# First edge stretch of a two-part graph kernel: stores of packed sums on two queues, each step's mix in two halves

## The chip, the cores and the metric

The kernel runs on one core of one Trainium2 chip. The metric is the device time of one execution in microseconds (us), as the median of several runs.

## What is computed

The input is 50,000 nodes with 128 features and 50,000 edges sorted by destination. The first part is a graph attention layer with four heads (below), then a normalisation over all nodes, an ELU, a residual and a layer norm. The second part is two relational layers over the same edges. The change touches the edge work of the first part alone.

```python
src = jnp.concatenate([edge_index[0], loop]); dst = jnp.concatenate([edge_index[1], loop])
xl = (x @ Wl).reshape(n, H, C);  xr = (x @ Wr).reshape(n, H, C)
m = xl[src] + xr[dst]
logits = jnp.einsum('ehc,hc->eh', jax.nn.leaky_relu(m, 0.2), att)
amax = jax.ops.segment_max(logits, dst, num_segments=n)
ex = jnp.exp(logits - amax[dst])
denom = jax.ops.segment_sum(ex, dst, num_segments=n)
out = jax.ops.segment_sum((ex / (denom[dst] + 1e-16))[:, :, None] * xl[src], dst, num_segments=n)
```

## The kernel before

The program is written by hand, one instruction list for each engine, with semaphores between them; the order of the lists is the order of the code. The work runs in stages. In the first, the node projections xl and xr are made for all nodes and written to DRAM; then comes the stretch that the change is about, the first edge stretch.

The edges are cut into four chains (`CHAINS`) of 100 (`ROWS`) tiles of 125 (`TE`). The stretch is a loop of 100 steps; step i takes tile i of each of the four chains. What one step does, by engine:

- GpSimd gathers the source rows of xl, one indirect transfer for each chain (L879), up to six steps ahead. It waits until `values` of six steps earlier has read the buffer.
- SyncE's queue loads four windows of 224 rows of xr (`load_windows`, L457 for the addresses, L461 for the transfers), three steps ahead; a step's buffers come free when its mix is done. Every fourth step it also loads a block of two tables (L618, L621). Then it stores the packed sums of an earlier step (`save_sums`, L429 for the addresses, L644 for the four transfers of 125 rows of 137 floats). The store of a chain waits until the store of the same chain a step earlier has landed (semaphore `ew_out`), since neighbouring tiles overlap in DRAM and the later one must win.
- TensorE runs `mix(i+1)`: for each chain one transpose of the gathered rows (L998) and two matmuls (L1000) that add the destination's rows, into one bank. Then come `logits(i)` (L1010), `compact(i-1)` (L1026), which sums the edges of a node, and `turn_back(i)` (L1016, L1017), which turns the maxima.
- VectorE builds the turned selection (L1732), runs the segment maxima (`maxima`, L1751 to L1758), the leaky ReLU (L1739), the values (L1769, L1770) and the slot matrix (L1721, L1723).
- ScalarE copies the mixed bank out (`edges_mixed`, L1270), copies the packed sums out (`compacted`, L1294), carries an open node's sum into the next tile (`carry`, L1285, L1286) and makes the gains (`gains`, L1278, L1279). `compacted(i)` also waits for the stores of three steps earlier, whose buffer it writes.

The packed sums carry from one step into the next: `values(i)` waits for `carry(i)`, which waits for `compacted(i-1)`. On TensorE the order of a step is

```python
for i in range(ROWS + 1):
    if i + 1 < ROWS:
        mix(i + 1)
    if i < ROWS:
        logits(i)
    if i:
        compact(i - 1)
    if i < ROWS:
        turn_back(i)
```

After the loop, the stage ends with three short joins of neighbouring chains (L684 to L686), which wait for all stores. The later stages are not touched.

Of the kernel before, what the change touches and what calls it, by code (L numbers as in the profile page):

```python
# [8 lines left out]
ALU = mybir.AluOpType  # L9
# [4 lines left out]
D = 128  # L14
# [44 lines left out]
CHAINS = 4  # L59
ROWS = 100  # L60
# [97 lines left out]
def gnn_kernel(nc, x, src, dst, etype, Wl, Wr, att, bias_conv, gn_weight, gn_bias, gn_mean_scale,  # L158
               basis, comp, loop_w, bias, out):
    ctx = ExitStack()  # L160
    with ctx:
# [265 lines left out]
        def addresses(eng, row, least=0):  # L427

            return nc.values_load_multi_w_load_instructions(  # L429
                row, engines=[eng.engine], min_val=least, max_val=N + CHAINS * GAP,  # L430
                skip_runtime_bounds_check_because="a rank is below the number of edges, plus a gap for each chain")[1]

        def gathered(i):
            return quad((0, 5)[i % 6 // 3], i % 3)
# [102 lines left out]
        def _(sp):  # L537
# [99 lines left out]
            def save_sums(i):  # L637
                sp.wait_ge(ec_cp, i + 1)
                if i == 0:
                    sp.wait_ge(zero_out, 16)  # L640
                for c, at in enumerate(addresses(sp, edge_at[i:i + 1, :])):
                    if i:
                        sp.wait_ge(ew_out[c], 16 * i)
                    sp.dma_start(w_d[0][bass.ds(at, TE), :], quad(3, i % 3, WIDE)[1:SLOTS, c, :]).then_inc(ew_out[c], 16)  # L644
# [305 lines left out]
        def _(pe):  # L950
# [36 lines left out]
                    last = pe.matmul(right[:, at], quad(10, q % 2)[:, t, :], w_lr[:, D:2 * D], start=True, stop=True)  # L987
                last.then_inc(qp_ps, 1)

            def mix(i):  # L990
                both = psum[i % 2]
                pe.wait_ge(e_in[i % 6], 64 * (i // 6 + 1))
                pe.wait_ge(window_in[i % 3], 64 * (i // 3 + 1))
                pe.wait_ge(pt_ok, i + 1)
                if i >= 2:
                    pe.wait_ge(m_cp, i - 1)
                for c in range(CHAINS):
                    pe.transpose(both[:, c * P:(c + 1) * P], gathered(i)[:, c, :], ident[:, :])  # L998
                    for h in range(2):
                        last = pe.matmul(both[:, c * P + 1:c * P + 1 + TE], window(c, i)[:, h, :],  # L1000
                                         turned_pick(h, i)[:, c, :], start=False, stop=h == 1, skip_group_check=True)
                last.then_inc(mx_ps, 1)

            def logits(i):
                pe.wait_ge(lr_ok, i + 1)
# [13 lines left out]
            def compact(i):  # L1019
                pe.wait_ge(es_ok, i + 1)  # L1020
                pe.wait_ge(v_ok, i + 1)
                if i:
                    pe.wait_ge(ec_cp, i)
                for c in range(CHAINS):
                    o = c % 2 * WIDE
                    last = pe.matmul(psum[5 + c // 2][0:SLOTS, o:o + WIDE], quad(4, i % 3, SLOTS)[:, c, :],  # L1026
                                     quad(2, i % 3, WIDE)[:, c, :], start=True, stop=True)
                last.then_inc(ec_ps, 1)
# [19 lines left out]
                    weigh(q // 3 - 1)  # L1048
            pe.wait_ge(ql_cp, QUADS)
            pe.wait_ge(qr_cp, QUADS)  # L1050
            mix(0)
            for i in range(ROWS + 1):
                if i + 1 < ROWS:
                    mix(i + 1)
                if i < ROWS:
                    logits(i)
                if i:
                    compact(i - 1)
                if i < ROWS:
                    turn_back(i)  # L1060
            end_stage(pe, 1)
# [164 lines left out]
        def _(act):  # L1226
# [61 lines left out]
            def compacted(i):  # L1288
# [6 lines left out]
                                          psum[5 + b][0:SLOTS, 0:2 * WIDE].rearrange("p (t d) -> p t d", d=WIDE), ACT.Copy)  # L1295
                last.then_inc(ec_cp, 1)

            def weighed(n):
                act.wait_ge(coef_ps, n + 1)
                act.activation(coef[:, 4 * n:4 * n + 4, :, :, :].rearrange("p i l c b -> p (i l c b)"),  # L1300
                               COEF[:, 0:BLOCK * RELS], ACT.Copy).then_inc(coef_cp, 1)
# [9 lines left out]
            for i in range(ROWS + 1):  # L1311
                if i + 1 < ROWS:
                    edges_mixed(i + 1)
                if i:
                    compacted(i - 1)
                if 0 < i < ROWS:
                    carry(i)
                if i < ROWS:
                    gains(i)
            for k in range(CHAINS - 1):  # L1320
                act.wait_ge(join_arg, k + 1)
                act.activation(join[:, 4:6, :], join[:, 2:4, :], ACT.Exp).then_inc(join_exp, 1)
# [199 lines left out]
        def _(dve):  # L1522
# [5 lines left out]
            def per_head(small):  # L1528

                a = small.unsqueeze(len(small.shape))  # L1530
                return a.to_broadcast(list(small.shape) + [C])
# [163 lines left out]
            def by_head(a):  # L1695
                return a.rearrange("p t (h c) -> p t h c", h=H)
# [63 lines left out]
            def values(i):  # L1760

                row = quad(2, i % 3, WIDE)
                ex = gains_ps[:, :, 0:H]
                dve.wait_ge(ex_ok, i + 1)
                if i:
                    dve.wait_ge(kept_ok, i)
                if i >= 3:
                    dve.wait_ge(ec_ps, i - 2)
                st.did(dve.tensor_tensor(by_head(row[:, :, 0:D]), by_head(gathered(i)), per_head(ex), ALU.mult))  # L1769
                st.did(dve.tensor_tensor(row[:, :, D:WIDE], gains_ps, factors[:, i, :, :], ALU.mult))  # L1770
                st.wait()
                dve.sem_inc(v_ok, 1)

            dve.memset(work[15][:, 0:WIDE], 0.0).then_inc(zero_ok, 1)
            for q in range(QUADS):
# [377 lines left out]
```

## Time and profile before

| | us |
|---|---|
| median of 3 runs | 3302.61 (3302.51 to 3315.04) |
| profiled execution, its own time | 3311.62 |
| its span | 3309.7 |
| TensorE busy | 2855.8 (86%) |
| VectorE busy | 2485.2 (75%) |
| GpSimd busy | 1721.9 (52%) |
| ScalarE busy | 1711.1 (52%) |

The first edge stretch is the part of the span from 355 to about 970 us. The shares of the table are means over stages with different limits, so the stretch is read by itself, with the views below restricted to it. In the views, L644 is line 644 of the kernel; SPq and ACTq are the queues' own instructions, in which SyncE and ScalarE issue transfers; PE, DVE, ACT and POOL are TensorE, VectorE, ScalarE and GpSimd. `w_d<-work` is a store of packed sums, `work<-xr_d` a load of a window, `work<-xl_d,slot_src` a gather, `work<-rel_d` the larger of the two tables.

### The profile page before, as it was taken

The page shows a single profiled execution, that of the slowest core. Times are in us where ns is not written, and L with a number is a line of the kernel's source. Part 1 is how long each engine was busy: PE and PEld are TensorE (multiplying, and loading weights), DVE is VectorE, ACT ScalarE, POOL GpSimd, SP SyncE. Part 2 cuts the span into 40 slices and gives each one's busy share as a digit, 9 for nine tenths or more (in the row PEclk, how much of TensorE's full clock was granted, in tenths as well). Part 3 has the DMA queues.
Part 4 walks back from the last instruction along what each step waited for, and adds up shares of the span by engine and source line. Part 5 has one row for each costly group of instructions (what it writes and reads, how often), then busy time and mean ns, then how long its engine had stood idle before and what let it go on. Part 6 is the DMA issues. An engine that isn't in the chain of part 4 may idle for free.

```text
span 3309.7 us, 64642 instructions
## 1 busy us (share of the span) xinstructions
PE 2855.8 (86%) x16643; PEld 2071.9 (63%) x16643; DVE 2485.2 (75%) x7657; ACT 1711.1 (52%) x4118; POOL 1721.9 (52%) x2037
## 2 busy tenths in 40 slices
PE   4998688888856888899799999979989999979897
PEld 4888577777744555688655555568855555546665
DVE  5999677666656899788677777734457777768998
ACT  2555233333323444699766666534446666645665
POOL 1220676666621222477777777612257777744554
PEclk9999899989988999899899999989999999999999
DMA  7999687877757887799533333369953333339997
GB/s 179 271 271 272 174 187 187 184 184 181 182 124 193 246 243 232 230 293 295 184 102 103 104 103 104 96 223 299 296 164 103 103 104 104 103 83 306 340 331 259
DMA packets 754301, 640.69 MB, mean 194 GB/s; under 512 B 75927, under 2 KB 631532, under 8 KB 753932
## 3 DMA queue, kind: packets, MB, share of 16 engines
q1 hardware_dynamic: 599874, 419.42, 45.2%
q0 software_dynamic: 54208, 130.20, 14.3%
q10 hardware_dynamic: 99850, 86.91, 8.1%
q8 instruction: 139, 2.28, 0.3%
q14 instruction: 230, 1.88, 0.2%
HBM read 402.00 MB, written 234.23 MB: 192 GB/s over the span
## 4 chain that ended last, share of the span: by engine, by line
POOL 24%; DVE 18%; issue 14%; DMA 12%; PE 10%; SPq 9%; ACT 8%; ACTq 3%; DVEq 0%; POOLq 0%
POOL work L921 23%; DMA w_d<-work 7%; ACT work L1397 4%; PE bank L1194 3%; PE bank L1201 3%; DMA work<-w_d 2%; SPq L461 2%; SPq L644 2%; DVE work L1779 2%; DVE work L1710 2%; DVE work L1712 2%; DVE self_logit L1714 2%; ACTq L468 1%; ACT work L1389 1%; SPq L429 1%
## 5 line engine op out<-in xcount | busy, mean ns | idle before, releaser
L2038 DVE SCALAR_TENSOR_TENSOR work<-bank,coef,work 128x128 f32<-128x128 f32 x2400 | 673.8, 342 | 245.8 <-ACT work L1431 242.0
L1147 PE MATMUL bank<-basis_s,work 128*128 128x512 f32 x1600 | 756.1, 596 | 1.5 <-ACT work L1424 1.5
L879 POOL DMA_INDIRECT work<-xl_d,slot_src x400 | 410.0, 1025 | 270.2 <-issue 193.2
L921 POOL DMA_INDIRECT work<-x_d,slot_src x400 | 385.4, 964 | 126.3 <-issue 121.6
L921 POOL DMA_INDIRECT work<-h_d,slot_src x400 | 383.9, 960 | 123.8 <-issue 121.6
L1431 ACT ACTIVATE work<-bank,coef 128x128 f32<-128x128 f32 x800 | 293.6, 367 | 226.7 <-PE bank L1147 226.7
L1147 PEld LDWEIGHTS bank<-basis_s,work 128*128 128x128 f32 x1600 | 274.5, 191 | 196.5 <-issue 192.5
L1158 PEld LDWEIGHTS bank<-work 128*126 128x126 f32 x1600 | 207.0, 189 | 101.7 <-issue 101.0
L1201 PEld LDWEIGHTS bank<-work 128*128 128x128 f32 x1552 | 206.3, 194 | 97.3 <-issue 92.7
L1000 PE MATMUL bank<-work 112*128 112x125 f32 x1600 | 255.6, 294 | 0.0
L893 POOL DMA_DIRECT2D conv_d<-work x99 | 73.8, 750 | 323.8 <-DVE work L1927 315.3
L1000 PEld LDWEIGHTS bank<-work 112*128 112x128 f32 x1600 | 240.4, 215 | 0.0
L1194 PE MATMUL bank<-work,loop_s 128*128 128x512 f32 x392 | 213.0, 626 | 31.1 <-ACT work L1471 30.2
L1138 PEld LDWEIGHTS bank<-ident,work 128*128 128x128 f32 x800 | 85.6, 142 | 209.6 <-DMA work<-x_d,slot_src 92.2
L1158 PE MATMUL bank<-work 128*126 128x128 f32 x1600 | 208.8, 273 | 5.7 <-ACT work L1437 3.4
L1471 ACT ACTIVATE work<-bank 128x512 f32<-128x512 f32 x196 | 114.7, 585 | 184.9 <-issue 159.5
L1201 PE MATMUL bank<-work 128*128 128x128 f32 x1552 | 207.5, 277 | 1.4 <-DMA work<-w_d 1.4
L998 PE MATMUL bank<-ident,work 128*128 128x128 f32 x400 | 121.7, 304 | 78.0 <-DMA work<-xr_d 54.1
L1084 PE MATMUL bank<-work,ones 128*128 128x512 f32 x392 | 179.2, 602 | 3.3 <-ACT work L1348 3.3
L938 POOL DMA_DIRECT2D h_d<-work x99 | 53.7, 543 | 246.5 <-DVE work L2072 242.6
L1270 ACT ACTIVATE work<-bank 128x512 f32<-128x512 f32 x100 | 59.7, 597 | 236.5 <-PE bank L1000 236.5
L1119 PE MATMUL bank<-work,ident 128*128 128x128 f32 (+1 forms) x782 | 162.1, 289 | 21.6 <-DVE work L1988 21.3
(271 smaller groups left out, 6513.7 us busy)
## 6 DMA issues: line engine op xcount, KB each, us to landing
w_d<-work SPq DMA_DIRECT2D x800, 62.5 KB
work<-in_x_dram SPq DMA_DIRECT2D x194, 256.0 KB, 4.2
work<-x_d SPq DMA_DIRECT2D x194, 256.0 KB, 4.5
work<-xr_d SPq DMA_DIRECT2D x400, 112.0 KB
w_d<-work SPq DMA_DIRECT2D x400, 66.9 KB
work<-w_d SPq DMA_DIRECT2D x398, 64.0 KB, 3.4
work<-w_d ACTq DMA_DIRECT2D x390, 64.0 KB, 3.4
xl_d<-work SPq DMA_DIRECT2D x97, 256.0 KB, 2.9
```

The source lines that it names most:

```text
L879: pool.indirect_dma_start(gathered(i)[:, c, :], None, xl_d, bass.IndirectOffsetOnAxis(ap=slot_src[:, a:a + 1], axis=0)).then_inc(e_in[i % ...
L921: pool.indirect_dma_start(quad(0, i % 3)[:, c, :], None, (x1_d, h1_d)[l], bass.IndirectOffsetOnAxis(ap=slot_src[:, a:a + 1], axis=0)).then ...
L1000: last = pe.matmul(both[:, c * P + 1:c * P + 1 + TE], window(c, i)[:, h, :], turned_pick(h, i)[:, c, :], start=False, stop=h == 1, skip_gr ...
L1084: last = pe.matmul(psum[b][:, 0:whole * D], ones[:, :], rows[:, 0:whole, :].rearrange("p t d -> p (t d)"), start=False, stop=False, skip_g ...
L1119: pe.matmul(to[0:rows, at], ident[0:rows, 0:rows], skip_rows(q)[0:rows, t, :], start=True, stop=False)
L1147: pe.matmul(psum[YBANKS[k % 5]][:, :], quad(1, i % 2)[:, c, :], basis_s[:, l, :, :].rearrange("k b n -> k (b n)"), start=True, stop=True). ...
L1158: last = pe.matmul(psum[5 + c // per_bank][0:SLOTS, o:o + width], quad(4, i % 3, SLOTS)[:, c, :], quad(2, i % 3, width)[:, c, :], start=Tr ...
L1194: pe.matmul(to[:, 0:m], loop_s[:, l, :], work[7][:, (q % 2) * 512:(q % 2) * 512 + m], start=True, stop=False, skip_group_check=True)
L1201: last = pe.matmul(at, packed(q, D)[:, t, :], sel.rearrange("r (t p) -> r t p", t=4), start=False, stop=t == n - 1, skip_group_check=True)
L1397: last = act.activation(quad(8, k)[0:rows, t, :], psum[2 + q % 4][0:rows, t * D:(t + 1) * D], ACT.Identity, bias=norm[0:rows, k, 1, t:t + ...
L1431: act.activation(quad(2, i % 3, width)[:, c, 0:D], psum[YBANKS[k % 5]][:, 0:D], ACT.Copy, scale=coef[:, i, l, c, 0:1]).then_inc(r["first"], 1)
L2038: ins = dve.scalar_tensor_tensor(o, psum[YBANKS[k % 5]][:, b * D:(b + 1) * D], coef[:, i, l, c, b:b + 1], o, ALU.mult, ALU.add)
```

## The change

The four stores of a step are shared: chains 0 and 1 stay on SyncE's queue, chains 2 and 3 go to ScalarE's, in a new `save_sums` at the end of ScalarE's step. The mix of a step is cut in two halves of two chains each: the first half of `mix(i+2)` runs between `compact(i-1)` and `turn_back(i)`, the second half after `turn_back(i)`, where the whole mix was. On VectorE, the two instructions of `values` no longer go through a counted wait of the engine on itself; the second one signals `v_ok`.

```diff
--- before.py
+++ after.py
@@ -638,7 +638,7 @@
                 sp.wait_ge(ec_cp, i + 1)
                 if i == 0:
                     sp.wait_ge(zero_out, 16)
-                for c, at in enumerate(addresses(sp, edge_at[i:i + 1, :])):
+                for c, at in zip(range(0, 2), addresses(sp, edge_at[i:i + 1, 0:2])):
                     if i:
                         sp.wait_ge(ew_out[c], 16 * i)
                     sp.dma_start(w_d[0][bass.ds(at, TE), :], quad(3, i % 3, WIDE)[1:SLOTS, c, :]).then_inc(ew_out[c], 16)
@@ -987,19 +987,21 @@
                     last = pe.matmul(right[:, at], quad(10, q % 2)[:, t, :], w_lr[:, D:2 * D], start=True, stop=True)
                 last.then_inc(qp_ps, 1)
 
-            def mix(i):
+            def mix(i, half):
                 both = psum[i % 2]
-                pe.wait_ge(e_in[i % 6], 64 * (i // 6 + 1))
-                pe.wait_ge(window_in[i % 3], 64 * (i // 3 + 1))
-                pe.wait_ge(pt_ok, i + 1)
-                if i >= 2:
-                    pe.wait_ge(m_cp, i - 1)
-                for c in range(CHAINS):
+                if half == 0:
+                    pe.wait_ge(e_in[i % 6], 64 * (i // 6 + 1))
+                    pe.wait_ge(window_in[i % 3], 64 * (i // 3 + 1))
+                    pe.wait_ge(pt_ok, i + 1)
+                    if i >= 2:
+                        pe.wait_ge(m_cp, i - 1)
+                for c in range(2 * half, 2 * half + 2):
                     pe.transpose(both[:, c * P:(c + 1) * P], gathered(i)[:, c, :], ident[:, :])
                     for h in range(2):
                         last = pe.matmul(both[:, c * P + 1:c * P + 1 + TE], window(c, i)[:, h, :],
                                          turned_pick(h, i)[:, c, :], start=False, stop=h == 1, skip_group_check=True)
-                last.then_inc(mx_ps, 1)
+                if half == 1:
+                    last.then_inc(mx_ps, 1)
 
             def logits(i):
                 pe.wait_ge(lr_ok, i + 1)
@@ -1048,14 +1050,18 @@
                     weigh(q // 3 - 1)
             pe.wait_ge(ql_cp, QUADS)
             pe.wait_ge(qr_cp, QUADS)
-            mix(0)
+            mix(0, 0)
+            mix(0, 1)
+            mix(1, 0)
             for i in range(ROWS + 1):
                 if i + 1 < ROWS:
-                    mix(i + 1)
+                    mix(i + 1, 1)
                 if i < ROWS:
                     logits(i)
                 if i:
                     compact(i - 1)
+                if i + 2 < ROWS:
+                    mix(i + 2, 0)
                 if i < ROWS:
                     turn_back(i)
             end_stage(pe, 1)
@@ -1295,6 +1301,15 @@
                                           psum[5 + b][0:SLOTS, 0:2 * WIDE].rearrange("p (t d) -> p t d", d=WIDE), ACT.Copy)
                 last.then_inc(ec_cp, 1)
 
+            def save_sums(i):
+                act.wait_ge(ec_cp, i + 1)
+                if i == 0:
+                    act.wait_ge(zero_out, 16)
+                for c, at in zip(range(2, 4), addresses(act, edge_at[i:i + 1, 2:4])):
+                    if i:
+                        act.wait_ge(ew_out[c], 16 * i)
+                    act.dma_start(w_d[0][bass.ds(at, TE), :], quad(3, i % 3, WIDE)[1:SLOTS, c, :]).then_inc(ew_out[c], 16)
+
             def weighed(n):
                 act.wait_ge(coef_ps, n + 1)
                 act.activation(coef[:, 4 * n:4 * n + 4, :, :, :].rearrange("p i l c b -> p (i l c b)"),
@@ -1317,6 +1332,8 @@
                     carry(i)
                 if i < ROWS:
                     gains(i)
+                if i:
+                    save_sums(i - 1)
             for k in range(CHAINS - 1):
                 act.wait_ge(join_arg, k + 1)
                 act.activation(join[:, 4:6, :], join[:, 2:4, :], ACT.Exp).then_inc(join_exp, 1)
@@ -1766,10 +1783,8 @@
                     dve.wait_ge(kept_ok, i)
                 if i >= 3:
                     dve.wait_ge(ec_ps, i - 2)
-                st.did(dve.tensor_tensor(by_head(row[:, :, 0:D]), by_head(gathered(i)), per_head(ex), ALU.mult))
-                st.did(dve.tensor_tensor(row[:, :, D:WIDE], gains_ps, factors[:, i, :, :], ALU.mult))
-                st.wait()
-                dve.sem_inc(v_ok, 1)
+                dve.tensor_tensor(by_head(row[:, :, 0:D]), by_head(gathered(i)), per_head(ex), ALU.mult)
+                dve.tensor_tensor(row[:, :, D:WIDE], gains_ps, factors[:, i, :, :], ALU.mult).then_inc(v_ok, 1)
 
             dve.memset(work[15][:, 0:WIDE], 0.0).then_inc(zero_ok, 1)
             for q in range(QUADS):
```

On TensorE, one step of the loop before, from `logits` (L1010) on (L1026 is `compact`, L1016 and L1017 `turn_back`, L998 and L1000 the mix):

```order
L1010 MATMUL bank<-work,att_heads 16x128 x4
L1026 MATMUL bank<-work 126x137 x4
L1016 MATMUL bank<-ident,exp_arg 128x16
L1017 MATMUL bank<-ident,seg_max 128x16
L998 MATMUL bank<-ident,work 128x128
L1000 MATMUL bank<-work 128x125 x2
```

The last two rows are the first chain of the mix; three more such pairs follow, then the next `logits`.

The same step now (L999 and L1001 are the mix, L1012 `logits`, L1028 `compact`, L1018 and L1019 `turn_back`):

```order
L1012 MATMUL bank<-work,att_heads 16x128 x4
L1028 MATMUL bank<-work 126x137 x4
L999 MATMUL bank<-ident,work 128x128
L1001 MATMUL bank<-work 128x125 x2
L999 MATMUL bank<-ident,work 128x128
L1001 MATMUL bank<-work 128x125 x2
L1018 MATMUL bank<-ident,exp_arg 128x16
L1019 MATMUL bank<-ident,seg_max 128x16
L999 MATMUL bank<-ident,work 128x128
L1001 MATMUL bank<-work 128x125 x2
```

Two pairs, which are two chains of the mix, have moved ahead of `turn_back`; the other two follow it, of which the first is shown. Nothing is added or taken away on TensorE.

On ScalarE, the step now, from the `gains` (L1284, L1285) to the next ones (L1276 is `edges_mixed`, L1300 `compacted`, L1291 and L1292 `carry`):

```order
L1285 ACTIVATE bank<-bank 128x4x4
L429 TENSOR_LOAD edge_at
L1311 ISA
L1311 DMA w_d<-work 125x137
L1311 ISA
L1311 DMA w_d<-work 125x137
L1276 ACTIVATE work<-bank 128x512
L1300 ACTIVATE work<-bank 126x274 x2
L1291 ACTIVATE work<-work 1x512
L1292 ACTIVATE factors<-work 1x4x4
L1284 ACTIVATE bank<-bank 128x4x4
```

The address load and the two stores stand between the gains and the next copy of a mixed bank; SyncE's list loses the same two stores a step.

## Rows read from the trace of the kernel before

**Rows 1.** Windows view, first edge stretch: busy us and instructions by engine, granted clock, DMA share, GB/s.

```profile
core 0: us, PE busy (x) PEld busy (x) DVE busy (x) ACT busy (x) POOL busy (x), PEclk, DMA share, GB/s
355.00:965.00 610.00, 512.46 (x3785) 443.35 (x3786) 424.74 (x1187) 208.65 (x690) 406.42 (x397) 0.94 0.77 182
```

**Rows 2.** Line view of the running maximum (VectorE, one per step): durations, first and last start.

```profile
L1752 DVE TENSOR_TENSOR_SCAN run_max<-drop_t,seg_max,bank x99: 451/452/454, 368.1 to 965.2; 16x125 f32<-16x125 f32 x99
```

**Rows 3.** Chain of waits, 360 to 960 us: shares by line; start, length, what.

```profile
by line: DMA w_d<-work 33.2%; SPq L461 11.4%; SPq L644 11.0%; issue 10.9%; SPq L457 6.7%; PE bank L1000 4.4%; DMA work<-xr_d 4.0%; POOL work L879 3.3%; SPq L429 2.2%; PE bank L1010 1.9%; PE bank L998 1.4%; SPq L621 1.3%; DVE work L1732 1.1%
...
606.22 7.69 DMA w_d<-work
...
645.49 6.21 DMA w_d<-work
```

**Rows 4.** Timeline of SyncE's queue, 685 to 696 us: start, length, engine, line, operation.

```profile
685.91 1.87 SPq L461 DMA_DIRECT2D work<-xr_d  x4
688.56 2.36 SPq L644 DMA_DIRECT2D w_d<-work  x4
691.94 1.87 SPq L461 DMA_DIRECT2D work<-xr_d  x4
694.34 1.70 SPq L644 DMA_DIRECT2D w_d<-work  x4
```

**Rows 5.** Line views of the address loads: durations min/median/max.

```profile
L457 SPq TENSOR_LOAD <-base_at x100: 298/818/2189, 344.6 to 950.9; - x100
...
L429 SPq TENSOR_LOAD <-edge_at x309: 274/466/867, 369.8 to 2973.8; - x155
L429 ACTq TENSOR_LOAD <-node_at x293: 278/912/1698, 997.3 to 3281.2; - x147
```

**Rows 6.** Timeline, two steps without a stall; in brackets the idle time before and its end.

```profile
650.70 0.60 ACT L1270 ACTIVATE work<-bank 128x512 f32<-128x512 f32 x1 [1.45 <-PE bank L1000]
...
653.16 0.67 DVE L1739 SCALAR_TENSOR_TENSOR work<-work 128x512 f32<-128x512 f32 x1
...
653.28 0.23 PE L1016 MATMUL bank<-ident,exp_arg 16*128 16x16 f32 x1 [0.51 <-DVE exp_arg L1758]
...
658.35 0.23 PE L1016 MATMUL bank<-ident,exp_arg 16*128 16x16 f32 x1 [0.29 <-DVE exp_arg L1758]
```

**Rows 7.** Timeline of TensorE in a stalled step.

```profile
666.61 0.45 PE L998 MATMUL bank<-ident,work 128*128 128x128 f32 x1 [2.35 <-DMA work<-xr_d]
```

**Rows 8.** Line view, 360 to 955 us: busy us, mean ns, idle before with its ends.

```profile
L879 POOL DMA_INDIRECT work<-xl_d,slot_src x389 | 399.0, 1026 | 184.3 <-issue 107.3 <-DVEq L1772 77.0
...
L1721 DVE TENSOR_TENSOR work<-bank,slot_row 128x500 f32<-128x500 f32 x97 | 65.9, 679 | 14.5 <-DVE work L1770 0.5
```

**Rows 9.** Waits, 360 to 955 us: who waited for whom, total us, times, longest.

```profile
ACT work L1270 <- PE bank L1000: 235.1, 99, 22.8
...
ACT work L1294 <- DMA w_d<-work: 55.4, 26, 3.9
PE bank L998 <- DMA work<-xr_d: 54.1, 43, 2.9
...
PE bank L1016 <- DVE exp_arg L1758: 39.0, 97, 1.3
```

**Rows 10.** Waits of SyncE's queue in the same stretch.

```profile
SPq L644 <- DMA w_d<-work: 33.2, 71, 1.3
```

**Rows 11.** Windows view: a stretch with stores in transfer, one with loads (columns of rows 1).

```profile
641.00:641.50 0.50, 0.01 (x1) 0.04 (x2) 0.00 (x0) 0.50 (x4) 0.37 (x1) 1.00 0.36 103
...
657.00:659.00 2.00, 1.35 (x10) 1.05 (x10) 1.82 (x6) 0.81 (x3) 1.44 (x2) 1.00 1.05 271
```

**Rows 12.** Timeline of SyncE's queue at the end of the stretch.

```profile
954.02 20.55 SPq L644 DMA_DIRECT2D w_d<-work  x24
978.91 0.38 SPq L684 DMA_DIRECT2D work<-w_d  x1
```


## Prediction, made before the changed kernel was run

> **What bounds the kernel now.** I read the stretch by itself, in this order: the windows view, the spacing of the steps, the chain of waits, SyncE's queue, and then the waits of each engine.
>
> The windows view shows no engine at its limit: TensorE is busy 512 of 610 us (84%), VectorE 70%, GpSimd 67%, ScalarE 34%, and the DMA engines have a share of 0.77 [rows 1]. The running maximum comes once a step; its 99 later starts lie between 368.1 and 965.2 us, so that a step takes 597.1 / 98 = 6.09 us on average [rows 2]. Two undisturbed steps follow each other in 658.35 - 653.28 = 5.07 us [rows 6]. So the engines can do a step in about 5.1 us, and on average about 1 us a step is lost to something else.
>
> The chain of waits says to what. Of the 600 us from 360 to 960, 33.2% are transfers of packed sums (`w_d<-work`), and the instructions of SyncE's queue (L461, L644, L457, L429, L621) take 11.4 + 11.0 + 6.7 + 2.2 + 1.3 = 32.6% more; the compute engines together have about an eighth. The long pieces of it are single stores that land 6.2 to 7.7 us after they were issued [rows 3], longer than a step. The queue's timeline shows why: four window loads, four stores, four window loads, with no pause [rows 4]. By the rows, a step costs SyncE 0.82 (window addresses) + 1.87 (four loads) + 0.47 (store addresses) + 1.70 (four stores) = 4.86 us when nothing holds it [rows 4, 5], and it is held: its stores wait 33.2 us for earlier stores [rows 10], and groups of four that should take 1.70 us take 2.36 [rows 4]. What is late then is the next window: TensorE waits for windows 54.1 us in all, up to 2.9 us at once [rows 9], as in the step at 666.61 us, where it stood still for 2.35 us [rows 7]. ScalarE waits another 55.4 us for stores to land before it may write their buffer [rows 9].
>
> **The change, part by part.**
>
> *Two stores a step leave SyncE's queue.* SyncE issues half of 1.70 us less, so its step falls from 4.86 to about 4.0 us. [...] At the end of the stretch, where no windows are loaded any more, 24 stores pass in 20.55 us, 0.86 us each [rows 12]. If the two queues' stores pass side by side, SyncE's queue is free of 2 x 0.86 = 1.71 us a step, and 6.09 - 1.71 = 4.38 us remain. If they share one resource, nothing is won and the step stays at 6.09. These are the two ends for the queues.
>
> *What is late next.* Before 4.38 is reached, another engine decides. A gather on GpSimd takes 1.026 us and 107.3 / 389 = 0.28 us of issue follows; the 77 us that it waits for `values` are not counted. Four of them make (399.0 + 107.3) / 389 x 4 = 5.21 us a step [rows 8]. GpSimd's list is unchanged, so 5.21 us is a floor for the step.
>
> *The value I take.* Between 5.21 and 6.09 I take 5.5. It lies nearer to GpSimd's row, because the DMA engines have room just where it is needed: while stores alone are in transfer, their share is 0.36 at 103 GB/s, while in a burst of loads it is 1.05 at 271 GB/s [rows 11]. The second queue can fill that room. But it is not all room: at 5.21 us a step the mean share would be 0.77 x 6.09 / 5.21 = 0.90, so I leave a third of the way. The gain is 98 x (6.09 - 5.50) = 58 us.
>
> *What ScalarE gets.* An address load, which on its queue takes 0.278, 0.912 or 1.698 us (least, median, most) [rows 5], and two stores at 1.70 / 4 = 0.43 us each: 1.1 to 2.6 us a step, 1.8 typically. It stands between the gains and the next copy of a mixed bank, where ScalarE waits for TensorE 235.1 / 99 = 2.4 us a step on average [rows 9] and 1.45 us in an undisturbed step [rows 6]. In a fast step the copy then comes some 0.3 us late; its reader L1739 starts at 653.16, 1.86 us after the copy that began at 650.70 has ended [rows 6], so this costs nothing. Without that cover it would be 0.3 us a step, 30 us. Behind the added waits on `ew_out` stand that copy, `compacted` and `carry`, and through these VectorE and GpSimd; the third rival prices that.
>
> *Half of the mix ahead of `turn_back`.* TensorE waits 39.0 / 97 = 0.40 us a step for the maxima [rows 9]; half a mix now fills that, and the floor of TensorE falls from 5.07 to about 4.7 us. Since GpSimd holds 5.21, this is worth nothing by itself: 0 to 0.1 us a step. In exchange the waits for windows and gathers now stand ahead of `turn_back`, so that a late window also delays the gains and the values. Those are needed by `compact`, which comes only after the second half of the mix and the logits; I put this at nothing as long as windows are in time.
>
> *VectorE's wait on itself.* VectorE is idle 14.5 / 97 = 0.15 us ahead of L1721 [rows 8], which is that wait. VectorE is busy 70% of the time; 0 to 0.15 us a step, off the path, taken as nothing.
>
> *The end of the stretch.* The last store is issued at 974.6, and the joins begin at 978.91 [rows 12]. Of the last four stores two pass on the other queue, 2 x 0.86 = 1.7 us earlier.
>
> The sum is 58 + 2 = 60 us. The profiled execution took 3311.6 us, so 3251.6 for one like it; it stood 9 us above the median of the three runs, 3302.6, and against that I forecast 3302.6 - 60 = **3243 us**.
>
> **The rivals.**
>
> *GpSimd's floor is reached.* For it: in undisturbed steps everything already runs in 5.07. Against it: a burst of tables every fourth step remains. At 5.21 us the gain is 98 x 0.88 + 2 = 88 us: 3214.
>
> *The stores share a few DMA engines, and the queue does not matter.* While stores alone are in transfer the share is 0.36 [rows 11], which is what five or six of the sixteen engines at full work would give. If a store of 125 rows uses only these, and they also have their part of windows, gathers and tables, then those few are busy through the whole step, and a second queue gives them no time. The step stays between 5.9 and 6.09, a gain of 0 to 19 us: 3284 to 3303, most likely 3299. For it speaks that queued stores pass at 0.86 us even with nothing beside them [rows 12]; against it, that SyncE's own instructions already fill 4.86 of the 6.09 us, so that part of the loss must be the queue's. [...]
>
> *ScalarE is held by its own stores.* Each of its stores waits for that chain's last one. In the chain stores land 6.21 us after issue and more [rows 3]. If they did so on the new queue, a step could not be shorter than 6.21 + 0.43 = 6.64 us, and here no slack of three window buffers lies between the wait and the compute chain: 98 x 0.55 = 54 us slower, 3357. It decides as soon as landings take longer than about 5.6 us. Against it: the new queue carries no windows, so a store finds at most one other ahead of it.
>
> **How the numbers follow.** My forecast, a step of 5.3 to 5.8 us (3223 to 3272), has a chance of 0.60; GpSimd's floor 0.12; the shared engines 0.20, of which 0.17 within half a per cent (16.5 us, about what a measurement of this kernel can tell from no change) and 0.03 beyond it; ScalarE held 0.08. Faster is 0.60 + 0.12 + 0.03 = 0.75, the same 0.17, slower 0.08. The range leaves out the held ScalarE, a part of the floor and the very end of the shared engines: 3216 to 3302.
>
> **What would show it.** Right: the spacing of the running maximum falls to about 5.5 us; SyncE's waits for stores (33.2 us) and TensorE's for windows (54.1 us) shrink to less than half; the DMA share of the stretch rises to 0.85 or more; GpSimd waits less for `values`; ScalarE shows its stores between gains and copy without VectorE waiting for the copy. The forecast is wrong if the spacing stays near 6.09 with the windows still late (shared engines), or if ScalarE's queue shows waits for `w_d<-work` as long as a store's landing and the copies come late (ScalarE held).

## The result, and the profile after

The changed kernel takes 3280.6 us in the median of four runs (3273.1 to 3284.0), the kernel before 3307.3 in four runs beside it. The ratio is 0.9913, with a 95% interval of 0.9894 to 0.9932: some 27 to 29 us, or 0.9%, faster. The forecast was 3243 us, a gain of 60, so the direction was right and the gain a little under half of what I said. The profiled execution took 3273.1 us, 38.5 less than the profiled one before (3311.6). The profiled execution before lay 9 us above the median of its kernel (3302.6) and this one 7.5 us below, so differences between the two traces are somewhat larger than the typical gain.

The windows view of the stretch, which is now 30 us shorter, answers to [rows 1], and the line view of the running maximum to [rows 2].

```profile
355.00:935.00 580.00, 510.20 (x3786) 437.20 (x3785) 406.44 (x1192) 206.43 (x692) 394.41 (x396) 0.95 0.81 192
```

```profile
L1769 DVE TENSOR_TENSOR_SCAN run_max<-drop_t,seg_max,bank x99: 450/452/453, 368.0 to 932.9; 16x125 f32<-16x125 f32 x99
```

A step takes (932.9 - 368.0) / 98 = 5.76 us; before it took 6.09. 98 times the difference is 32 us. The joins, which follow the stretch, begin at 945.88 instead of 978.91 [rows 12], 33.0 us earlier. So the gain lies in the stretch. The other 5.5 us between the two profiled executions lie behind it, where the kernels are the same; I count them to no part of the change. The mean DMA share rose only from 0.77 to 0.81, where I had asked for 0.85.

The chain of waits from 360 to 930 us, with the shares by line and two of its pieces (start, length, what), answers to [rows 3]:

```profile
by line: DMA w_d<-work 51.2%; PE bank L1001 8.5%; issue 7.1%; DMA work<-xr_d 5.6%; PE bank L1028 4.5%; PE bank L1012 4.1%; PE bank L999 3.3%; SPq L461 3.2%; POOL work L879 2.9%; SPq L644 1.6%; SPq L457 1.5%; ACT work L1300 1.3%; SPq L429 1.
...
403.01 5.40 DMA w_d<-work
...
732.95 8.09 DMA w_d<-work
```

SyncE's own instructions, 32.6% of the chain before, are down to 3.2 + 1.6 + 1.5 + about 1 = 7%. What took their place are the stores themselves: 51% where it was 33%. The long pieces are still single stores that land 5 to 8 us after issue. The landing of its stores is now the largest part of what holds the step; no other owner has more than 8.5%.

The waits from 360 to 920 us (who waited for whom, total us, times, longest) answer to [rows 9], and those of SyncE's queue to [rows 10]:

```profile
ACT work L1276 <- DMA w_d<-work: 286.5, 89, 5.7
...
POOL work L879 <- DVE work L1787: 58.3, 43, 4.0
DVE work L1756 <- ACT work L1276: 46.5, 43, 2.8
...
PE bank L999 <- issue: 36.2, 34, 2.5
...
PE bank L999 <- DMA work<-xr_d: 18.4, 18, 3.3
...
ACT work L1300 <- DMA w_d<-work: 10.0, 6, 3.0
...
PEld bank L1018 <- DVE exp_arg L1775: 0.2, 1, 0.2
```

```profile
SPq L644 <- DMA w_d<-work: 76.4, 77, 2.7
```

Two of my signs came, and a wait that I had expected to fill went: TensorE waits for windows 18.4 us instead of 54.1 (and stands another 36.2 us ahead of the same transposes for nothing that the profile names; the mix waits there for ScalarE's copy too, so the late copy is likely, but not shown), GpSimd waits 58.3 us for `values` instead of 77.0, and TensorE no longer waits for the maxima (39.0 before, 0.2 now, of the weight load). Besides the DMA share, these did not come: SyncE's waits for stores grew from 33.2 to 76.4 us, and ScalarE stands 286.5 us in front of its copy of the mixed bank (L1276, L1270 before), because the two stores that are issued ahead of that copy wait for the landing of the row before. VectorE, which needs the copy, waits 46.5 us for it (L1756). The timeline of ScalarE shows one such step (ACTq is its queue; in brackets the idle time and its end):

```profile
646.97 0.12 ACT L1285 ACTIVATE bank<-bank 128x16 f32<-128x16 f32 x1
649.65 1.89 ACTq L1311 DMA_DIRECT2D w_d<-work  x2
651.92 0.60 ACT L1276 ACTIVATE work<-bank 128x512 f32<-128x512 f32 x1 [4.83 <-DMA w_d<-work]
652.41 0.68 ACT L1300 ACTIVATE work<-bank 126x274 f32<-126x274 f32 x2
```

The gains are done at 647.09, and the first of the two stores is issued only at 649.65. The copy begins at 651.92, 4.83 us after the gains. This is the mechanism of my third rival, at a chance of 0.08. After this result three theories stood: the queue of ScalarE holds the step through its order waits; few DMA engines are full and everything else only waits for them; or the halves of the mix eat what the queues win.

### The profile page after: what moved, and what is told of

Same layout as the page of the kernel before. It is cut to its first block, busy times and chain, and to the rows that moved or that the text cites. A ratio compares the mean times of both kernels' runs of the same rounds, so it can differ in the third digit from the quotient of the medians.

```text
span 3271.3 us, 64645 instructions
## 1 busy us (share of the span) xinstructions
PE 2862.2 (87%) x16643; PEld 2069.6 (63%) x16643; DVE 2466.4 (75%) x7657; ACT 1709.4 (52%) x4118; POOL 1707.3 (52%) x2037
## 3 DMA queue, kind: packets, MB, share of 16 engines
q0 software_dynamic: 54208, 130.20, 14.4%
## 4 chain that ended last, share of the span: by engine, by line
POOL 24%; DVE 17%; DMA 15%; PE 15%; issue 13%; ACT 9%; ACTq 4%; SPq 2%; DVEq 0%; POOLq 0%
POOL work L921 23%; DMA w_d<-work 10%; ACT work L1414 4%; PE bank L1200 4%; PE bank L1207 3%; DMA work<-w_d 2%; DVE work L1727 2%; DVE work L1794 2%; DVE work L1729 2%; DVE self_logit L1731 2%; ACTq L468 2%; PE bank L1001 1%; ACT work L1406 1%; PE bank L1220 1%; PE bank L1174 1%
## 5 line engine op out<-in xcount | busy, mean ns | idle before, releaser
L879 POOL DMA_INDIRECT work<-xl_d,slot_src x400 | 398.8, 997 | 249.9 <-issue 191.6
L1001 PE MATMUL bank<-work 112*128 112x125 f32 x1600 | 249.3, 286 | 0.0
L1001 PEld LDWEIGHTS bank<-work 112*128 112x128 f32 x1600 | 233.8, 209 | 0.0
L1276 ACT ACTIVATE work<-bank 128x512 f32<-128x512 f32 x100 | 59.7, 597 | 331.8 <-DMA w_d<-work 291.9
L999 PE MATMUL bank<-ident,work 128*128 128x128 f32 x400 | 121.9, 305 | 81.9 <-issue 36.2
```

The costliest lines, as they stand in the source:

```text
L879: pool.indirect_dma_start(gathered(i)[:, c, :], None, xl_d, bass.IndirectOffsetOnAxis(ap=slot_src[:, a:a + 1], axis=0)).then_inc(e_in[i % ...
```

## The experiments

Every time below is the median of its runs, and every ratio is against the kernel before on the same chip. The step is the spacing of the running maximum. The windows of the views end earlier where the stretch does.

**The split alone.** The first kernel takes from the change only `save_sums` on two queues; the mix stays whole.

```
-                for c, at in enumerate(addresses(sp, edge_at[i:i + 1, :])):
+                for c, at in zip(range(0, 2), addresses(sp, edge_at[i:i + 1, 0:2])):
...
+            def save_sums(i):
+                act.wait_ge(ec_cp, i + 1)
...
+                if i:
+                    save_sums(i - 1)
```

> The split of the stores alone (chains 2 and 3 on ScalarE's queue), with the mix whole, as before, and VectorE's counted wait kept. Queue theory (the stores' own queue held the step): it gives nearly all that the change gave, 20 to 30 us below the kernel before. Engine theory (a store of 125 rows uses only five of the DMA engines, which both queues share): the step is still held by those engines, 0 to 30 us, no more than the change. If the order on TensorE was what gained, this gives under 10 us. All theories: ScalarE's queue waits for w_d<-work, over 200 us in the stretch.

Measured: 3270.8 us, ratio 0.9918 [0.9896, 0.9940]. Line view of the running maximum and waits from 360 to 920 us:

```profile
L1763 DVE TENSOR_TENSOR_SCAN run_max<-drop_t,seg_max,bank x99: 451/452/453, 367.6 to 930.3; 16x125 f32<-16x125 f32 x99
```

```profile
ACT work L1270 <- DMA w_d<-work: 193.9, 61, 5.9
...
PE bank L1016 <- DVE exp_arg L1769: 51.4, 97, 1.7
```

A step takes 562.7 / 98 = 5.74 us. The split gives the whole gain of the change. TensorE still waits for the maxima here (51.4 us), so the order on TensorE is not what gained. Between the queue and the engines this run does not decide: both theories allowed about this time. ScalarE's wait, 193.9 us, is just short of the 200 that I had put down for all of them.

**The halves alone.** The second kernel takes from the change only the two halves of the mix.

```
-            def mix(i):
+            def mix(i, half):
...
-                    mix(i + 1)
+                    mix(i + 1, 1)
...
+                if i + 2 < ROWS:
+                    mix(i + 2, 0)
```

> The halved mix alone, all four stores on SyncE's queue, VectorE's counted wait kept. Queue theory and engine theory: the stores are as before, so the time is as before, within 8 us; TensorE's wait for the maxima (39 us) goes, and its waits for windows take its place. If the order on TensorE was what gained: 20 to 30 us below.

Measured: 3301.7 us, ratio 0.9996 [0.9982, 1.0010]. Line view:

```profile
L1758 DVE TENSOR_TENSOR_SCAN run_max<-drop_t,seg_max,bank x99: 451/452/453, 366.8 to 956.4; 16x125 f32<-16x125 f32 x99
```

A step takes 589.6 / 98 = 6.02 us. The halves are worth nothing where the stores bind. In this run, too, the maxima no longer hold TensorE (0.2 us), and that therefore explains nothing of the gain. The profiled execution took 3302.1 us, 9.6 us less than the profiled one before, though the medians agree; 6.02 is thus the step of a typical execution with the stores as before, and 6.09 that of a slightly long one.

**Stores of 126 rows, one queue.** If a store of 125 rows runs on few engines because of its number of rows, one row more is the smallest edit that changes it. Here the kernel before is made to store 126 rows of every tile instead of 125; the extra row is zero and is overwritten by the next row's store, like the other rows that overlap. The matrix `pick`, the matmul of `compact` and the copy get one column or row more.

```
+SAVED = 126
+PICKS = SAVED + 1
...
-                    sp.dma_start(w_d[0][bass.ds(at, TE), :], quad(3, i % 3, WIDE)[1:SLOTS, c, :]).then_inc(ew_out[c], 16)
+                    sp.dma_start(w_d[0][bass.ds(at, SAVED), :], quad(3, i % 3, WIDE)[1:PICKS, c, :]).then_inc(ew_out[c], 16)
```

> The kernel before, with each store made 126 rows in place of 125 (a 127th column of zeros in the slot matrix gives the further row; the later tile overwrites it), all on SyncE's queue. Engine theory: 126 rows spread over fourteen engines, a store passes in about a third of 0.86 us, its wait goes, and the step falls from 6.1 to about 5.3 us, GpSimd's pace: 60 to 85 us below the kernel before, more than the change gave. Queue theory (stores pass one after the other whatever their rows): 0.8% more bytes, 0 to 8 us above the kernel before.

Measured: 3281.4 us, ratio 0.9940 [0.9919, 0.9961]. Line view; chain of waits from 360 to 940 us; SyncE's queue from 690 to 710 us:

```profile
L1754 DVE TENSOR_TENSOR_SCAN run_max<-drop_t,seg_max,bank x99: 451/452/454, 366.9 to 944.2; 16x125 f32<-16x125 f32 x99
```

```profile
by line: DMA w_d<-work 21.0%; SPq L646 17.4%; SPq L463 17.2%; issue 13.5%; SPq L459 6.1%; PE bank L1002 4.5%; DMA work<-xr_d 3.8%; SPq L431 3.2%; PE bank L1012 2.0%; SPq L623 1.6%; PE bank L1000 1.5%; PE bank L1028 1.4%; SPq L620 1.4%; DVE 
```

```profile
694.93 1.87 SPq L463 DMA_DIRECT2D work<-xr_d  x4
698.39 1.93 SPq L646 DMA_DIRECT2D w_d<-work  x4
701.31 1.87 SPq L463 DMA_DIRECT2D work<-xr_d  x4
703.71 1.93 SPq L646 DMA_DIRECT2D w_d<-work  x4
```

A step takes 577.3 / 98 = 5.89 us, 20 us less in all; I had expected 60 to 85. Here the picture of the changed kernel is reversed: the stores' share of the chain fell from 33.2% to 21.0%, and SyncE's instructions (L646, L463, L459, L431, L623, L620) rose from 32.6% to 46.9%. A group of four stores now takes 1.93 us, where four that nothing held took 1.70 and held ones 2.36 [rows 4]. Now that the stores are less in the way, SyncE's queue is the largest owner of the chain, though the stores still have a fifth of it.

**Stores of 126 rows, two queues.** The same edit in the changed kernel, on both queues.

> The changed kernel with stores of 126 rows. Engine theory: 60 to 90 us below the kernel before, as the same edit without the change or a little lower; ScalarE's waits for w_d<-work fall from 286 us to under 50. Queue theory: as the changed kernel, 27 us below the kernel before, ScalarE still waiting.

Measured: 3239.1 us, ratio 0.9810 [0.9788, 0.9831]. Line view; chain of waits and one wait from 360 to 890 us:

```profile
L1771 DVE TENSOR_TENSOR_SCAN run_max<-drop_t,seg_max,bank x99: 451/452/454, 367.3 to 897.3; 16x125 f32<-16x125 f32 x99
```

```profile
by line: POOL work L881 68.5%; issue 21.0%; DMA work<-xl_d,slot_src 3.7%; DMA w_d<-work 3.0%; PE bank L1003 1.0%; PE bank L1001 0.5%; PE bank L1030 0.4%; ACT work L1302 0.4%; PE bank L1014 0.4%; SPq L463 0.3%; SPq L646 0.2%; SPq L431 0.1%; 
```

```profile
ACT work L1278 <- DMA w_d<-work: 194.7, 90, 5.4
```

A step takes 530.0 / 98 = 5.41 us. The stores have left the chain (3.0%), and GpSimd's gathers and the issue between them are 90% of it: GpSimd sets the pace here, as in my first rival. ScalarE still waits 194.7 us for landings, where the engine theory said under 50; that sign missed. The wait is now hardly on the path (3.0%). Why ScalarE still waits that long was not followed.

**Stores of 127 rows.** The last edit once more with `SAVED = 127`, a number that only one divides.

> The changed kernel with stores of 127 rows. Theory A (a transfer is spread over the largest number of engines up to 16 that divides its rows: five for 125, fourteen for 126, one for the prime 127): all stores run through a single engine. 4 x 127 rows of some 29 ns make 14.7 us a step and up to 18 with its share of the windows, so the stretch grows by 900 to 1250 us: 4150 to 4550 us. Rival B (126 rows gained for another reason, such as rows that are merely more or a different alignment): 3240 to 3300 us.

Measured: 4459.7 us in one run. Line view, and the windows view of 2 us in which only stores are in transfer (columns of rows 1):

```profile
L1771 DVE TENSOR_TENSOR_SCAN run_max<-drop_t,seg_max,bank x99: 450/452/453, 366.7 to 2069.9; 16x125 f32<-16x125 f32 x99
```

```profile
1002.00:1004.00 2.00, 0.00 (x0) 0.00 (x0) 0.00 (x0) 0.00 (x0) 0.00 (x0) 0.50 0.07 17
```

A step takes 1703.2 / 98 = 17.4 us, and the share is 0.07, which is 1.1 of sixteen engines. One row more than 126 costs 1221 us. For 125 and 126 rows the same view can be read at the end of the stretch, where neither windows nor gathers are in transfer any more. The rows are the kernel before (125 rows, one queue), the changed kernel (125 rows, two queues) and the split kernel with 126 rows that follows below (two queues):

```profile
956.00:975.00 19.00, 9.43 (x73) 7.76 (x71) 12.68 (x40) 5.83 (x21) 0.00 (x0) 0.87 0.31 79
```

```profile
926.00:934.00 8.00, 6.18 (x44) 5.15 (x44) 5.99 (x19) 2.32 (x11) 0.00 (x0) 0.93 0.28 68
```

```profile
884.50:885.00 0.50, 0.50 (x5) 0.44 (x4) 0.50 (x1) 0.00 (x0) 0.00 (x0) 1.00 0.90 241
```

With 125 rows the share over 19 us is 0.31, or 5.0 of sixteen engines; the 0.36 of [rows 11] was a mean over half a microsecond. With two queues, each of which moved about half, it is 0.28 or 4.5: two queues together keep no more engines at work than one did, so both use the same ones. The window of the 127 rows says the same: packets of both queues are in it, 32 and 31, and together they have the time of 1.1 engines (3.5% of sixteen each). They pass at 2 us / 63 = 32 ns a packet, where theory A had some 29; the 98 packets in the half microsecond of [rows 11] took 0.36 x 16 x 0.5 / 98 = 29 ns each. With 126 rows the share reaches 0.90, or 14.4, in half a microsecond; so short a window makes this the roughest of the three. So the number of rows decides how many engines are at work while only stores are in transfer: 5.0 with 125, 14.4 with 126 and 1.1 with 127. Theory A said five, fourteen and one, and the time of the 127 rows lies in its range. That is shown for these three numbers of rows; no other was run.

**Without the order waits.** A store of the changed kernel overlaps the one before it, and so waits for it. Here the stores of rows of odd number go to a second tensor, on both queues, so that none overlaps the one before, and only the copy into the buffer waits. It waits for the stores of two rows earlier, where the changed kernel waits for those of three, so the edit takes one wait away and makes another tighter. The sums of the odd rows are missing from what is read later, so that the stretch alone can be compared. The lines below are ScalarE's half.

```
-                    if i:
-                        act.wait_ge(ew_out[c], 16 * i)
-                    act.dma_start(w_d[0][bass.ds(at, TE), :], quad(3, i % 3, WIDE)[1:SLOTS, c, :]).then_inc(ew_out[c], 16)
+                    act.dma_start((w_d[0], odd_d)[i % 2][bass.ds(at, TE), :], quad(3, i % 3, WIDE)[1:SLOTS, c, :]).then_inc(ew_out[2 + i % 2], 16)
```

> The changed kernel (stores of 125 rows, two queues), but rows of odd number go to a second tensor in DRAM, so that a store no longer overlaps the one before it and needs no wait for it; a buffer is only waited for at the copy two rows later. The tensor that is read afterwards thus lacks the sums of every odd row (zeros are written there ahead of the stretch, on ScalarE's queue, which adds some time before it): the output is not the reference's. So the spacing of the running maximum in the stretch decides, not the total. Theory A (a store of 125 rows uses few DMA engines, and those are full): the spacing stays within 0.15 us of the changed kernel's 5.76 us, 5.6 to 5.9; the waits move from the stores to the copies. Rival B (the wait of each store for the landing of its chain's last store is what holds ScalarE and SyncE): the spacing falls to GpSimd's 5.2 to 5.4 us.

Measured: 3408.6 us, with the zeros that are written ahead; the stretch itself by the line view, and waits from 510 to 1070 us:

```profile
L1774 DVE TENSOR_TENSOR_SCAN run_max<-drop_t,seg_max,bank x99: 450/452/454, 518.5 to 1069.2; 16x125 f32<-16x125 f32 x99
```

```profile
ACT work L1301 <- DMA w_d<-work: 107.7, 40, 5.2
...
ACT work L1301 <- DMA odd_d<-work: 56.6, 35, 2.5
```

A step takes 550.7 / 98 = 5.62 us: the exchange is worth 0.14 us of the 5.76. ScalarE now waits 164 us in front of `compacted`, for stores issued two rows before. With a row more of room than the order waits left, the stores still don't all land in time. How much the order waits alone are worth, with the buffer wait at three rows, was not tried, so 0.14 us may be too little. That they are not the main limit follows from the other side: the stores of 126 rows kept every one of them, and the step fell by 0.35 us.

**Both without the halves.** The kernel that the first results point to has the split and 126 rows, with the mix whole.

> The kernel before with the stores split over both queues and widened to 126 rows, the mix whole and the counted wait of VectorE kept. The changed kernel with 126 rows took 3239 us at GpSimd's pace. Theory A (halves of the mix and the missing wait of VectorE are worth nothing even when the stores are out of the way): 3232 to 3247 us. Rival B (with the stores out of the way TensorE's wait for the maxima counts, about 0.4 us a step): 3260 to 3280 us.

Measured: 3223.5 us, ratio 0.9770 [0.9754, 0.9787], the fastest of all. I had expected what the halved mix gave, or more. Line view and, from 360 to 880 us, the chain of waits; then GpSimd's gathers (busy us, mean ns, idle before) of this kernel and of the changed one with 126 rows:

```profile
L1765 DVE TENSOR_TENSOR_SCAN run_max<-drop_t,seg_max,bank x99: 450/451/453, 369.8 to 885.2; 16x125 f32<-16x125 f32 x99
```

```profile
by line: POOL work L881 34.9%; issue 15.8%; DMA w_d<-work 13.4%; PE bank L1002 5.1%; ACT work L1296 3.1%; PE bank L1028 2.9%; PE bank L1012 2.7%; DVE work L1745 2.5%; SPq L463 2.3%; ACTq L431 2.2%; DVE work L1782 2.0%; PE bank L1000 1.7%; D
```

```profile
L881 POOL DMA_INDIRECT work<-xl_d,slot_src x391 | 388.5, 994 | 119.2 <-issue 119.2
```

```profile
L881 POOL DMA_INDIRECT work<-xl_d,slot_src x385 | 403.0, 1047 | 117.4 <-issue 115.9 <-DVE work L1789 1.5
```

A step takes 515.4 / 98 = 5.26 us. By these rows GpSimd needs (388.5 + 119.2) / 391 x 4 = 5.19 us a step here, and (403.0 + 115.9) / 385 x 4 = 5.39 with the halves. In the halved kernel GpSimd is the bound, with 90% of the chain. In this one its gathers never wait, but the chain names them and the issue for only half of it, and the stores still for 13.4%: the step is at GpSimd's pace, and other limits lie close to it. Two parts of the change could do that, the halves and the counted wait of VectorE that the change drops, so three more kernels ran on one chip: this one without the counted wait, the halved one with it, and this one again.

> Split stores of 126 rows, the mix whole, VectorE's counted wait ahead of v_ok taken away (the other way round than in the next run). Split with 126 rows and the whole mix took 3223 us with gathers of 0.994 us on GpSimd; with halved mix and without the counted wait it took 3239 with gathers of 1.047 us. Theory A (the halves cost the 16 us: they put TensorE's wait for a gather ahead of turn_back): 3219 to 3229 us, gathers near 0.99 us. Rival B (the missing counted wait costs them: the last product follows the first at once, and gathers that run beside it get longer): 3233 to 3243 us, gathers near 1.04 us.

> Split stores of 126 rows, the mix in halves as in the change, VectorE's counted wait kept. Theory A (the halves cost the 16 us): 3233 to 3243 us, gathers near 1.04 us. Rival B (the missing counted wait costs them): 3219 to 3229 us, gathers near 0.99 us.

> The kernel with split stores of 126 rows, whole mix and counted wait once more, beside the two others on one chip: 3219 to 3229 us by either theory. If it comes out at 3235 or above, the difference of 16 us to the halved mix lies in the chip or the run and not in the kernel.

Measured, in this order: 3234.2 us, ratio 0.9791 [0.9771, 0.9811]; 3238.9 us, 0.9805 [0.9787, 0.9823]; 3230.9 us, 0.9777 [0.9760, 0.9794]. Line views of the three, and their gathers from 360 to 880 us:

```profile
L1765 DVE TENSOR_TENSOR_SCAN run_max<-drop_t,seg_max,bank x99: 450/452/453, 369.6 to 893.4; 16x125 f32<-16x125 f32 x99
L1771 DVE TENSOR_TENSOR_SCAN run_max<-drop_t,seg_max,bank x99: 450/452/454, 366.1 to 897.4; 16x125 f32<-16x125 f32 x99
L1765 DVE TENSOR_TENSOR_SCAN run_max<-drop_t,seg_max,bank x99: 450/452/453, 370.5 to 893.2; 16x125 f32<-16x125 f32 x99
```

```profile
L881 POOL DMA_INDIRECT work<-xl_d,slot_src x391 | 388.1, 992 | 125.7 <-issue 116.6 <-DVE work L1783 9.0
L881 POOL DMA_INDIRECT work<-xl_d,slot_src x386 | 402.1, 1042 | 117.8 <-issue 116.2 <-DVEq L1791 1.5
L881 POOL DMA_INDIRECT work<-xl_d,slot_src x390 | 391.4, 1004 | 121.4 <-issue 118.6 <-DVEq L1785 2.8
```

The steps are 5.34, 5.42 and 5.33 us, the gathers 0.992, 1.042 and 1.004 us. The times do not settle it as cleanly as the expectations asked: the first kernel has the gathers of theory A and a time in the range of rival B, the second fits theory A in both, and the third, expected at 3229 at most, came out 2 us above. The length of the gathers goes with the halves in all five kernels with 126 rows and two queues (0.99 to 1.00 us with the mix whole, 1.04 to 1.05 halved), whatever the counted wait does. With 125 rows it does not: there it is 1.03 us in the kernel before and 1.00 in the changed one. In time the halves cost some 8 us on this chip and 16 by the runs before it, which were on two chips. On this chip every run of the halved kernel (3233.1 us at least) was slower than every run of the same kernel with the mix whole and the wait kept (3231.2 at most), so the sign is likely; the size stays open, since the kernel that ran twice differs by 7 us between its two medians. What the counted wait is worth can't be told from zero. Nor is it shown that the longer gathers are what costs the time: in the two kernels with the mix whole on this chip GpSimd's own need, 5.16 and 5.23 us by the rows, is 0.1 to 0.2 us below the step, and stores still have 37% and 27% of their chains from 360 to 880 us. What lengthens a gather was not tried.

## Why the prediction was right in direction and wrong in size

*What bounds the kernel.* Right as far as it went: the queue of SyncE and the landing of the stores share the chain, and the split takes SyncE's instructions from 32.6% of it to 7%. What I missed is that these are two limits of nearly the same height, each with its own edit. The four steps show it:

| step, us (time, us) | stores of 125 rows | stores of 126 rows |
|---|---|---|
| one queue | 6.09 (3302) | 5.89 (3281) |
| two queues, mix whole | 5.74 (3271) | 5.26 (3223); again 5.33 (3231) |

Either edit alone wins 0.20 or 0.35 us a step, both win 0.76 to 0.83; in time 21 or 31 us, and 71 to 78.

*The value I take.* This is the step that failed. I took 5.5 us between 5.21 and 6.09 because "the DMA engines have room just where it is needed", from a share of 0.36 while stores are in transfer; measured were 5.76 (5.74 for the split alone). The term was 98 x 0.59 = 58 us, and came out as 98 x 0.33 = 32 between the two traces. The step of 5.76 is just inside my 5.3 to 5.8, but the time of 3280.6 is above the 3223 to 3272 that I had set beside it: I had counted the steps of an execution 9 us longer than the median against that median. The share is a mean over sixteen engines. A store of 125 rows uses about five of them, and while stores alone are in transfer these five are all at work (0.31 over the last 19 us, 5.0 of sixteen). The row that I read as room showed those five without any. The second queue could add stores only to the same five, and the two queues together kept 4.5 at work. What this means for a whole step can be estimated from ScalarE's queue in the changed kernel, which carries half of the stores and nothing else (packets, MB and share of 16 engines from 400 to 880 us):

```profile
q10 hardware_dynamic: 21465, 11.31, 9.1%
```

All stores then have about 0.18 of sixteen engines, which is 0.58 of five. The rest of the mean share, 0.81 - 0.18 = 0.63, comes on top if it is spread evenly over the sixteen (not shown here): about 1.2, so that the five are asked for more than all of their time, while the other eleven are at 0.63. That a few engines are busy through the whole step stood in my own second rival, and I gave it 0.20 because SyncE's instructions fill 4.86 of 6.09 us, as if one limit excluded the other.

*The lower end of 4.38 us.* It supposed that two queues pass stores side by side, and that each store holds its queue for 0.86 us. No run shows the second: 0.86 us is how far apart the last stores of the stretch were issued, when each also waited for its chain's last one to land. The first did not come. With 125 rows both queues use the same five engines (5.0 at work with one queue, 4.5 with two): stores still take up to 8.09 us to land, and SyncE waits for them 76.4 us instead of 33.2.

*The shared engines (second rival).* The mechanism was right; its time, 3284 to 3303 and likeliest 3299, was not quite. Its sentence "a second queue gives them no time" goes too far: the split won some 30 us. That SyncE's queue had kept the five engines from full use, and that this is the part that the split won, is argued from the two chains and not shown by a run. The issue time was not small here: with stores of 126 rows the split is worth 3281 - 3223 = 58 us (50 by the second run of that kernel), and SyncE's instructions were 46.9% of the chain of the kernel without it.

*ScalarE held by its own stores (third rival).* Half right. The waits are there, 286.5 us of them, and VectorE waits for the late copy. But they did not make the kernel slower, and the run without order waits prices them, against a tighter buffer wait, at 0.14 us a step, 14 us in all. With 126 rows ScalarE waits 194.7 us at GpSimd's pace, and stores have 3.0% of the chain. I take the wait as mostly the place where the late landing shows. Nor did it help that on the new queue "a store finds at most one other ahead of it": the engines, which both queues share, were what it found occupied.

*What ScalarE gets, VectorE's counted wait.* Taken as nothing. For the counted wait that stands: its effect can't be told from zero. The work that ScalarE gets was not measured by itself. Of the 2 us at the end of the stretch some 0.7 came: the joins begin 13.0 us after the last running maximum instead of 13.7.

*Half of the mix.* Taken as nothing by itself, and 0.9996 [0.9982, 1.0010] confirms it where the stores bind. That it likely costs something, 8 to 16 us in these runs, once the stores are wide and on two queues I had not seen.

*GpSimd's floor (first rival).* The floor of 5.21 us held: no kernel went below it, and with stores of 126 rows its own rows make it 5.16 to 5.39 us, depending on how long its gathers take. The change does not reach it; the split with 126 rows comes to it, at 5.26 us a step and 3223 us in one run and 5.33 and 3231 in the other, against 3214 worked out.

## What to carry to other kernels

A mean share of the DMA engines says little about room for a transfer that uses only some of them: read the share while that transfer is alone, times sixteen, and read it with another number of rows too (here 5.0 with 125, 14.4 with 126 and 1.1 with 127). One row more can be worth nearly as much as another queue (here 21 and 31 us), and both together more than their sum (71 to 78). When the chain of waits names two owners with a third each, price the removal of each with the other still there.

## What the runs showed of the hardware

Three things I had not expected. One more row per store, 126 instead of 125, takes 71 to 78 us off the kernel before together with a second queue, and 127 rows add some 1,180 us to the changed kernel; while stores alone are in transfer, about 14, 5 and 1 of the sixteen engines are at work with 126, 125 and 127 rows. A store of 126 rows is slower to issue than one of 125, 1.93 us for four against 1.70, so that the gain of the wider store is partly paid back on the queue that issues it. And the duration of a gather on GpSimd is no constant: its mean went from 0.99 to 1.05 us between kernels with the same list of gathers, which is 0.2 us for the four of a step. What sets it was not found.
